# A gated graph network on one core: the late block sums of the matrix as single passes between the first step's gate operations, and waits per bank at the head of step 0

## The chip, the cores and the metric

The kernel runs on 1 core of one Trainium2 chip. The metric is the device time of one execution in microseconds (us). A core has a matrix engine (PE, with weight loads listed apart as PEld), a vector engine (DVE), a scalar engine (ACT), a general engine (POOL) and a queue engine that starts transfers (SP). Each works through its own instructions in order and meets the others only at semaphores.

## The reference

```python
Af, AfT = A.astype(float32), A.astype(float32).T          # 2048 x 2048, zeros and ones
for _ in range(5):
    s_in, s_out = state @ in_W.T + in_b, state @ out_W.T + out_b      # state: 2048 x 256
    a_in, a_out = Af @ s_in, AfT @ s_out
    a = concatenate([a_in, a_out, state], axis=-1)
    r = sigmoid(a @ r_W.T + r_b)
    z = sigmoid(a @ z_W.T + z_b)
    h_hat = tanh(concatenate([a_in, a_out, r * state], axis=-1) @ h_W.T + h_b)
    state = (1.0 - z) * state + z * h_hat
out = tanh(state @ o1_W.T + o1_b) @ o2_W.T + o2_b
x = layernorm(x + out)
```

## The kernel before

The input weights are folded into the gate weights at the start, so a step needs only the products of A and of its transpose with the state, and the bias part of them is the row and column sums of A ("degrees") times a vector. All operands of PE are a high and a low f16 part, made by a `..._hi` operation on ACT and a `..._lo` operation on DVE.

**Streaming, step 0's products.** SP loads 32 row blocks of 1 MB, 16 of A and 16 of its transpose, into a ring of three stages (`load_rows`, k = 0 to 31). ACT casts each to fp8 into `areg` (`cast_rows`), which also gives the degrees. PE multiplies each block with the state into all eight banks. The blocks 14 and 15 of a matrix are kept for last and done bank by bank. For the transpose, column slice c and feature half f have the bank `p0_bank(c, f)`: banks 4, 5, 6, 7, 0, 1, 2, 3 in order. Each is emptied by `p0_hi` (before: the loop at L397 to L399) and `p0_lo` (L659). Between them PE spreads the degrees (`spread_degrees`, L1058) as one row each over banks 4 to 7, d = 0 for A and d = 1 for the transpose. `deg_out` (L719) copies them to `deg`.

**Gates.** A step has four column slices c of 512 nodes; n = 4 t + c counts them over steps. A slice has six gate tiles gi: two of r, two of z, two of h, each 18 matmuls of 128x512 on the banks 4, 5, 6 in turn (`gate_bank`). A bank is seeded with its degree parts first, one by ACT (`seed`, L451) and one by DVE (`degree_part`, L755, which releases the tile through `s_c1`). `gate_act` (L437) applies the sigmoid or tanh; `reset_part`, `reset_lo`, `keep_part` and `update` (L778, L781) are DVE's. `split_hi` (L408) and `split_lo` (L730) make the state operand of a slice, which its first tile needs. In step 0 PE turns finished slices around between tiles (`transposes`, L1176), and ACT and DVE make row operands of them (`rows_hi`, `row_sums`, `rows_lo` L737).

**Steps 1 to 4** multiply in blocks with seven products instead of eight, in four `group`s a step (L1075, 112 matmuls each). For these the matrix blocks' sums and differences are needed. `matrix_sums(i)` makes them on DVE, four passes (L651, L652, L654, L656) for each of 16 jobs; POOL stores them to `kept`. Eleven jobs stand in the streaming stage, the last five (`GATE_JOBS`) in step 0: one before the first `update` of each slice, the fifth after slice 3. SP loads a group's operands from `kept` into `areg` by `load_group`. The load for group 1 of step 1 waits until all sixteen jobs are stored.

The matmuls of groups 0 and 1, then the gates of slices 0 and 1, then groups 2 and 3 and slices 2 and 3 follow in each step. Behind the last slice stand its output head (`last_split_hi` L487, `last_split_lo` L845, `head_hidden` L1188, `head_out` L1207) and the layer norm.

## Time and profile before

| | |
|---|---|
| runs of the kernel before | 1072.14, 1072.59, 1076.05 us (median 1072.59) |
| profiled execution | 1071.97 us, its span 1070.0 us |
| PE busy | 1026.6 us, 96% |
| DVE, ACT busy | 594.9 us (56%), 414.5 us (39%) |
| POOL busy | 37.3 us (3%) |
| transfers | 119.63 MB |

The busy time says how long an engine had an instruction in work, not that it was needed then. The span runs from the first to the last instruction of the profile; 1.97 us of the profiled execution lie around it. Idle time of PE stands in brackets at the row that ends it, with what released it.

### The profile page before, as it was taken

The page shows a single profiled execution, that of the slowest core. Times are in us where ns is not written, and L with a number is a line of the kernel's source. Part 1 is how long each engine was busy: PE and PEld are TensorE (multiplying, and loading weights), DVE is VectorE, ACT ScalarE, POOL GpSimd, SP SyncE. Part 2 cuts the span into 40 slices and gives each one's busy share as a digit, 9 for nine tenths or more (in the row PEclk, how much of TensorE's full clock was granted, in tenths as well). Part 3 has the DMA queues.
Part 4 walks back from the last instruction along what each step waited for, and adds up shares of the span by engine and source line. Part 5 has one row for each costly group of instructions (what it writes and reads, how often), then busy time and mean ns, then how long its engine had stood idle before and what let it go on. Part 6 is the DMA issues. An engine that isn't in the chain of part 4 may idle for free.

```text
span 1070.0 us, 11716 instructions
## 1 busy us (share of the span) xinstructions
PE 1026.6 (96%) x4776; PEld 474.3 (44%) x4776; DVE 594.9 (56%) x924; ACT 414.5 (39%) x551; POOL 37.3 (3%) x44
## 2 busy tenths in 40 slices
PE   7999979998799999999999999999999999999994
PEld 3444434444344444444444444444444444444442
DVE  5999857777335336643543474344337544446755
ACT  3665545543124215521421462244126413322442
POOL 0311000000000000000000000000000001101100
PEclk9999989999899999999999999999999999999997
DMA  9999960000730033004103300330240035001101
GB/s 337 394 384 385 386 244 20 20 20 21 294 138 1 1 138 138 1 17 177 83 1 138 138 1 1 138 138 1 100 176 1 1 138 182 1 1 40 40 1 40
DMA packets 28869, 119.63 MB, mean 112 GB/s; under 512 B 2064, under 2 KB 17040, under 8 KB 20624
## 3 DMA queue, kind: packets, MB, share of 16 engines
q1 hardware_dynamic: 25968, 109.98, 26.8%
q0 software_dynamic: 2304, 8.39, 2.0%
q8 instruction: 37, 0.61, 0.2%
q10 hardware_dynamic: 544, 0.52, 0.1%
q14 instruction: 16, 0.13, 0.0%
HBM read 102.11 MB, written 16.78 MB: 111 GB/s over the span
## 4 chain that ended last, share of the span: by engine, by line
PE 88%; DVE 4%; DMA 2%; ACT 2%; issue 2%; SPq 1%; ACTq 0%; DVEq 0%
PE bank L1163 41%; PE bank L1075 34%; PE bank L1018 10%; PE bank L1176 1%; DMA areg<-kept_operands 1%; DMA tmp<-in_adj 1%; PE bank L1207 1%; PE bank L1188 1%; ACT xop_words L429 0%; DVE deg_words L719 0%; DVE tmp L654 0%; DVE tmp L652 0%; DVE tmp L651 0%; SPq L245 0%; ACT bank L451 0%
## 5 line engine op out<-in xcount | busy, mean ns | idle before, releaser
L1075 PE MATMUL bank<-areg,xop_words 128*128 128x512 fp8e4 x1792 | 392.9, 381 | 6.8 <-DMA areg<-kept_operands 5.4
L1163 PE MATMUL bank<-pq_words,w 128*128 128x512 f16 x1440 | 328.9, 380 | 0.0
L1075 PEld LDWEIGHTS bank<-areg,xop_words 128*128 128x128 f16 x1792 | 175.0, 98 | 219.8 <-DMA areg<-kept_operands 5.9
L1163 PEld LDWEIGHTS bank<-pq_words,w 128*128 128x128 f16 x1440 | 141.3, 98 | 170.0 <-issue 2.5
L437 ACT ACTIVATE tmp<-bank,bias_sb,scal 128x512 f32<-128x512 f32 x120 | 93.3, 777 | 219.7 <-PE bank L1163 211.4
L1163 PE MATMUL bank<-split,w 128*128 128x512 f16 x480 | 119.2, 385 | 11.4 <-DVE split L730 6.8
L755 DVE SCALAR_TENSOR_TENSOR bank<-deg_words,vdeg,bank 128x512 f32<-128x512 f16 x120 | 90.0, 752 | 63.5 <-ACT bank L451 62.3
L517 ACT ACTIVATE pq_words<-pq_words 128x512 f16<-128x512 f32 x48 | 30.2, 630 | 237.1 <-DVE pq_words L925 140.8
L1018 PE MATMUL bank<-areg,xop_words 128*128 128x512 fp8e4 x512 | 113.5, 383 | 2.7 <-ACT areg L377 2.7
L451 ACT ACTIVATE bank<-deg_words,vdeg 128x512 f32<-128x512 f16 x120 | 82.7, 691 | 5.4 <-DVE deg_words L719 1.7
L1018 PEld LDWEIGHTS bank<-areg,xop_words 128*128 128x128 f16 x512 | 50.0, 98 | 65.5 <-issue 7.7
L1163 PEld LDWEIGHTS bank<-split,w 128*128 128x128 f16 x480 | 47.2, 99 | 66.0 <-issue 9.5
L377 ACT ACTIVATE areg<-tmp 128x2048 fp8e4<-128x2048 int32 x32 | 61.1, 1911 | 38.5 <-DMA tmp<-in_adj_t 21.9
L761 DVE TENSOR_TENSOR tmp<-tmp,state_t 128x512 f32<-128x512 f32 x40 | 27.6, 691 | 62.2 <-ACT tmp L437 62.1
L1163 PE MATMUL bank<-tmp,w 128*128 128x512 f16 x240 | 58.3, 379 | 0.0
L939 DVE SCALAR_TENSOR_TENSOR pq_words<-pq_words 128x512 f16<-128x512 f32 x48 | 33.2, 692 | 33.4 <-ACT pq_words L517 33.4
L737 DVE SCALAR_TENSOR_TENSOR xop_words<-pq_words,scal,xop_words 128x512 f16<-128x512 f32 (+1 forms) x32 | 36.8, 1150 | 25.0 <-ACT xop_words L429 25.0
L778 DVE TENSOR_TENSOR tmp<-tmp 128x512 f32<-128x512 f32 x40 | 27.8, 694 | 37.4 <-ACT tmp L437 37.4
L360 POOL TENSOR_TENSOR areg<-areg,diag_words 128x256 f32<-128x256 f32 x16 | 14.2, 918 | 731.3 <-DMA areg<-in_x 731.3
L730 DVE SCALAR_TENSOR_TENSOR split<-state_t,scal,split 128x1024 f16<-128x1024 f32 x23 | 29.5, 1284 | 13.0 <-ACT split L408 12.8
L1163 PEld LDWEIGHTS bank<-tmp,w 128*128 128x128 f16 x240 | 23.5, 98 | 28.3
L429 ACT ACTIVATE xop_words<-pq_words,scal 128x512 f16<-128x512 f32 (+1 forms) x32 | 33.1, 1036 | 7.0 <-DVE pq_words L750 6.5
(118 smaller groups left out, 619.6 us busy)
## 6 DMA issues: line engine op xcount, KB each, us to landing
areg<-kept_operands SPq DMA_DIRECT2D x32, 1792.0 KB, 10.7
tmp<-in_adj SPq DMA_DIRECT2D x16, 1024.0 KB, 6.9
tmp<-in_adj_t SPq DMA_DIRECT2D x16, 1024.0 KB, 8.8
kept_operands<-xop_words POOLq DMA_DIRECT2D x11, 512.0 KB, 8.6
areg<-in_x SPq DMA_DIRECT2D x8, 512.0 KB, 8.0
kept_operands<-areg SPq DMA_DIRECT2D x4, 1024.0 KB, 9.6
kept_operands<-tmp POOLq DMA_DIRECT2D x5, 512.0 KB, 3.1
pq_words<-in_gate_w SPq DMA_DIRECT2D x6, 384.0 KB, 5.8
```

The costliest lines, as they stand in the source:

```text
L377: nc.scalar.activation(raw8[k // JT][:, k % JT, :], stage[:, k % STG, :], ACT.Copy, accum_out=degc[:, k // JT, k % JT:k % JT + 1], saturat ...
L429: nc.scalar.activation(xop[:, xs, 0, 2 * c:2 * c + 2, :], stg[:, bs, :], ACT.Identity, scale=SIGX) \
L437: nc.scalar.activation(dst[:, gi % FT, :], gate_bank[gi % 3][:, :], ACT.Tanh if gi >= 2 * FT else ACT.Sigmoid, bias=bias_sb[:, 4 + gi:5 + ...
L451: nc.scalar.activation(gate_bank[gi % 3][:, :], deg[:, 0, cols(c)], ACT.Identity, scale=vdeg[:, 0, gi:gi + 1]).then_inc(s_c0, 1)
L517: nc.scalar.activation(dst, src, ACT.Copy, scale=PSC / XDOWN).then_inc(s_yh, 1)
L730: nc.vector.scalar_tensor_tensor(split[:, c % 2, 1, :, :], state_t[:, :, cols(c)], SIG, split[:, c % 2, 0, :, :], ALU.mult, ALU.subtract). ...
L737: nc.vector.scalar_tensor_tensor(xop[:, xs, 1, 2 * c:2 * c + 2, :], stg[:, bs, :], SIGX, xop[:, xs, 0, 2 * c:2 * c + 2, :], ALU.mult, ALU. ...
L755: nc.vector.scalar_tensor_tensor(slot, deg[:, 1, cols(c)], vdeg[:, 1, gi:gi + 1], slot, ALU.mult, ALU.add).then_inc(s_c1, 1)
L939: nc.vector.scalar_tensor_tensor(rows[:, 1, :], src, PSC / XDOWN, rows[:, 0, :], ALU.mult, ALU.subtract).then_inc(s_yl, 1)
L1018: return nc.tensor.matmul(dst[:, :], state_n[:, j, part, feat(f)], adj8[:, j, cols(c)], start=j == 0 and part == 0, stop=j == JT - 1 and p ...
L1075: last = nc.tensor.matmul(dst[:, :], xop[:, xo, part, m, :], slot8[g % 2][:, m, mo, :], start=first and m == pairs[0] and part == 0, stop= ...
L1163: last = nc.tensor.matmul(dst[:, :], w16[:, k, wp, feat(gi)], rhs, start=False, stop=i == KT - 1 and (wp, xp) == PASSES[-1], skip_group_ch ...
```

## The change

It has five parts. (1) In `matrix_sum` the four passes of a late job stand apart, and `late_sum` puts them singly at five places of each slice's DVE operations in step 0, 20 passes in 20 places; all five jobs now end inside slice 3. (2) The first `split_hi(0, 0, 0)` stands in ACT's cast stream behind block 26 and its `split_lo` before `make_diag(1)`. (3) The degree rows of A are copied by ACT, those of the transpose by DVE, with a semaphore each (`s_deg_in`, `s_deg_out`), and seeds wait for the copy of their own bank; the banks of slices 2 and 3 are emptied after the seeds. (4) The load of `ow` stands behind block 12 instead of block 17. (5) In the last slice `last_split_hi(0)` stands before the last tile's activation instead of behind it.

```diff
--- before.py
+++ after.py
...
-                if k == JT + 1:
+                if k == JT - 4:
                     sp.dma_start(ow, o_w.rearrange("(k p) m -> p k m", p=P)).then_inc(s_ow, 16)
...
-            for k in range(JT + 1, 2 * JT):
-                cast_rows(k)
-            for c in range(CH):
-                for f in range(FT):
-                    act.wait_ge(s_p0, 2 * c + f + 1)
-                    nc.scalar.activation(pq[:, c, f, 0, :], bank[p0_bank(c, f)][:, :], ACT.Copy, scale=PSC) \
-                        .then_inc(s_p0h, 1)
...
             def split_hi(c, at, new):
+                if at == 0:
+                    for f in range(FT):
+                        act.wait_ge(s_xt[f], 32)
...
-                    if t == LAST and c == CH - 1 and gi == 5:
-                        last_split_hi(0)
-                        last_split_hi(1)
+                    if t == LAST and c == CH - 1 and gi >= 4:
+                        last_split_hi(gi - 4)
...
+            def p0_hi(c, f):
+                act.wait_ge(s_p0, 2 * c + f + 1)
+                nc.scalar.activation(pq[:, c, f, 0, :], bank[p0_bank(c, f)][:, :], ACT.Copy, scale=PSC) \
+                    .then_inc(s_p0h, 1)
+
+            for k in range(JT + 1, 2 * JT):
+                cast_rows(k)
+                if k == JT + 10:
+                    split_hi(0, 0, 0)
             act.wait_ge(s_bias, 16)
-            act.wait_ge(s_deg, 2 * CH)
+            for c in range(CH // 2):
+                for f in range(FT):
+                    p0_hi(c, f)
+            for c in range(CH):
+                act.wait_ge(s_dg, c + 1)
+                nc.scalar.copy(deg[:, 0, cols(c)], bank[4 + c][:, :]).then_inc(s_deg_in, 1)
+            act.wait_ge(s_deg_in, CH)
             for gi in range(3):
+                act.wait_ge(s_deg_out, gi + 1)
                 seed(0, 0, gi)
-            for f in range(FT):
-                act.wait_ge(s_xt[f], 32)
-            split_hi(0, 0, 0)
+            for c in range(CH // 2, CH):
+                for f in range(FT):
+                    p0_hi(c, f)
             for c in range(CH):
                 gates(0, c)
...
-            def matrix_sums(i):
+            def matrix_sum(i, which):
...
-                dve.wait_ge(s_cast, JT * d + 2 * m + 2)
...
-                nc.vector.tensor_tensor(t1, even[:, :, 1, :], even[:, :, 0, :], ALU.subtract, saturate=False).then_inc(s_tc, 1)
-                nc.vector.tensor_tensor(t3, odd[:, :, 1, :], even[:, :, 1, :], ALU.subtract, saturate=False)
-                dve.wait_ge(s_tc, 2 * i + 1)
-                nc.vector.tensor_tensor(t2, odd[:, :, 1, :], t1, ALU.subtract, saturate=False).then_inc(s_tc, 1)
-                dve.wait_ge(s_tc, 2 * i + 2)
-                nc.vector.tensor_tensor(t4, odd[:, :, 0, :], t2, ALU.subtract, saturate=False).then_inc(s_t, 1)
+                if which == 1:
+                    dve.wait_ge(s_cast, JT * d + 2 * m + 2)
+                    if 3 <= i < RING_A:
+                        dve.wait_ge(s_kept_a[i % 3], 16 * (i // 3))
+                    if i >= RING_A + 2:
+                        dve.wait_ge(s_kept_b[(i - RING_A) % 2], 16 * ((i - RING_A) // 2))
+                    nc.vector.tensor_tensor(t1, even[:, :, 1, :], even[:, :, 0, :], ALU.subtract, saturate=False) \
+                        .then_inc(s_tc, 1)
+                if which == 3:
+                    nc.vector.tensor_tensor(t3, odd[:, :, 1, :], even[:, :, 1, :], ALU.subtract, saturate=False)
+                if which == 2:
+                    dve.wait_ge(s_tc, 2 * i + 1)
+                    nc.vector.tensor_tensor(t2, odd[:, :, 1, :], t1, ALU.subtract, saturate=False).then_inc(s_tc, 1)
+                if which == 4:
+                    dve.wait_ge(s_tc, 2 * i + 2)
+                    nc.vector.tensor_tensor(t4, odd[:, :, 0, :], t2, ALU.subtract, saturate=False).then_inc(s_t, 1)
...
+            def late_sum(n, place):
+                k = 5 * n + place
+                if k < 4 * GATE_JOBS:
+                    matrix_sum(RING_A + k // 4, (1, 3, 2, 4)[k % 4])
...
-            for i in range(PAIRS, RING_A):
-                matrix_sums(i)
-            make_diag(1)
-
-            def p0_lo(c, f):
-                dve.wait_ge(s_p0h, 2 * c + f + 1)
-                lo_of_psum(c, f, bank[p0_bank(c, f)], s_p0l)
-
-            def deg_out(d):
-                for c in range(CH):
-                    dve.wait_ge(s_dg, CH * d + c + 1)
-                    nc.vector.tensor_copy(deg[:, d, cols(c)], bank[4 + c][:, :]).then_inc(s_deg, 1)
-
-            for c in range(CH):
-                p0_lo(c, 0)
-                if c >= CH - 2:
-                    deg_out(c - (CH - 2))
-                p0_lo(c, 1)
-            dve.wait_ge(s_deg, 2 * CH)
-
             def split_lo(c, at):
                 dve.wait_ge(s_sph, at + 1)
                 nc.vector.scalar_tensor_tensor(split[:, c % 2, 1, :, :], state_t[:, :, cols(c)], SIG,
                                                split[:, c % 2, 0, :, :], ALU.mult, ALU.subtract).then_inc(s_spl, 1)
...
+            for i in range(PAIRS, RING_A):
+                matrix_sums(i)
+            split_lo(0, 0)
+            make_diag(1)
+
+            def p0_lo(c, f):
+                dve.wait_ge(s_p0h, 2 * c + f + 1)
+                lo_of_psum(c, f, bank[p0_bank(c, f)], s_p0l)
+
+            for c in range(CH // 2):
+                for f in range(FT):
+                    p0_lo(c, f)
+            for c in range(CH):
+                dve.wait_ge(s_dg, CH + c + 1)
+                nc.vector.tensor_copy(deg[:, 1, cols(c)], bank[4 + c][:, :]).then_inc(s_deg_out, 1)
+            dve.wait_ge(s_deg_out, CH)
...
                 reset_lo(n, 0)
                 between(0)
+                if t == 0:
+                    late_sum(n, 0)
...
                 reset_lo(n, 1)
                 between(1)
+                if t == 0:
+                    late_sum(n, 1)
                 degree_part(n, c, 5)
...
                 if t == 0 and c + 1 < CH:
                     split_lo(c + 1, split_at(t, c + 1))
                 between(3)
+                if t == 0:
+                    late_sum(n, 2)
                 keep_part(n, c, 1)
                 if t == 0:
-                    for i in range(RING_A + c, RING_A + c + 1):
-                        matrix_sums(i)
+                    late_sum(n, 3)
                 if t == LAST and c == CH - 1:
                     head_split(2)
                 update(n, c, 0)
                 between(4)
                 if ahead:
                     degree_part(n + 1, (c + 1) % CH, 1)
+                if t == 0:
+                    late_sum(n, 4)
                 if c == CH - 1 and t < LAST:
                     rows_lo(n, 0)
...
             for gi in range(3):
                 degree_part(0, 0, gi)
-            split_lo(0, 0)
+            for c in range(CH // 2, CH):
+                for f in range(FT):
+                    p0_lo(c, f)
             for c in range(CH):
                 gates(0, c)
-                if c == CH - 1:
-                    for i in range(RING_A + CH, len(TJOBS)):
-                        matrix_sums(i)
...
                         pe.wait_ge(s_p0h, c + 1)
                         pe.wait_ge(s_p0l, c + 1)
                     else:
-                        pe.wait_ge(s_deg, c + 1)
+                        pe.wait_ge(s_deg_in, c + 1)
...
                 if n == 0 and f == 0:
-                    pe.wait_ge(s_deg, 2 * CH)
+                    pe.wait_ge(s_deg_out, CH)
...
```

The first place is the head of step 0 on DVE. Before, from `make_diag(1)` (L665) on, DVE has the parts of the products' banks (L659), both sets of degree rows (L719), the three degree parts of the gate banks (L755) and the split (L730) in this order:

```order
L665 TENSOR_SCALAR tmp<-ident,degc 128x128 x16
L659 SCALAR_TENSOR_TENSOR pq_words<-bank,pq_words 128x512 x5
L719 CAST deg_words<-bank 128x512 x4
L659 SCALAR_TENSOR_TENSOR pq_words<-bank,pq_words 128x512 x2
L719 CAST deg_words<-bank 128x512 x4
L659 SCALAR_TENSOR_TENSOR pq_words<-bank,pq_words 128x512
L755 SCALAR_TENSOR_TENSOR bank<-deg_words,vdeg,bank 128x512 x3
L730 SCALAR_TENSOR_TENSOR split<-state_t,scal,split 128x1024
```

In the changed kernel the same place reads:

```order
L735 SCALAR_TENSOR_TENSOR split<-state_t,scal,split 128x1024
L690 TENSOR_SCALAR tmp<-ident,degc 128x128 x16
L684 SCALAR_TENSOR_TENSOR pq_words<-bank,pq_words 128x512 x4
L752 CAST deg_words<-bank 128x512 x4
L777 SCALAR_TENSOR_TENSOR bank<-deg_words,vdeg,bank 128x512 x3
L684 SCALAR_TENSOR_TENSOR pq_words<-bank,pq_words 128x512 x4
```

The split moved ahead of everything, four of the eight degree copies are gone from DVE, and four of the eight bank parts moved behind the three degree parts.

The second place is the same one on ACT. Before:

```order
L377 ACTIVATE areg,degc<-tmp 128x2048 x15
L399 ACTIVATE pq_words<-bank 128x512 x8
L451 ACTIVATE bank<-deg_words,vdeg 128x512 x3
L408 ACTIVATE split<-state_t,scal 128x1024
L437 ACT_TABLE_LOAD
```

And in the changed kernel:

```order
L377 ACTIVATE areg,degc<-tmp 128x2048 x10
L403 ACTIVATE split<-state_t,scal 128x1024
L377 ACTIVATE areg,degc<-tmp 128x2048 x5
L532 ACTIVATE pq_words<-bank 128x512 x4
L545 CAST deg_words<-bank 128x512 x4
L446 ACTIVATE bank<-deg_words,vdeg 128x512 x3
L532 ACTIVATE pq_words<-bank 128x512 x4
L432 ACT_TABLE_LOAD
```

The split stands between the casts, the copies of the first degree rows came over from DVE, and half of the banks are emptied behind the seeds.

The third place is slice 1 of step 0 on DVE, from the split of slice 2 to the degree part (bank 5) that the second gate tile of slice 2 waits for. Before:

```order
L730 SCALAR_TENSOR_TENSOR split<-state_t,scal,split 128x1024
L737 SCALAR_TENSOR_TENSOR xop_words<-pq_words,scal,xop_words 128x5x256
L772 SCALAR_TENSOR_TENSOR tmp<-tmp,state_t 128x512
L651 TENSOR_TENSOR tmp<-areg 128x2x512
L652 TENSOR_TENSOR tmp<-areg 128x2x512
L654 TENSOR_TENSOR tmp<-areg,tmp 128x2x512
L656 TENSOR_TENSOR tmp<-areg,tmp 128x2x512
L778 TENSOR_TENSOR tmp<-tmp 128x512
L781 TENSOR_TENSOR state_t<-tmp 128x512
L755 SCALAR_TENSOR_TENSOR bank5<-deg_words,vdeg,bank5 128x512
```

In the changed kernel:

```order
L735 SCALAR_TENSOR_TENSOR split<-state_t,scal,split 128x1024
L759 SCALAR_TENSOR_TENSOR xop_words<-pq_words,scal,xop_words 128x5x256
L671 TENSOR_TENSOR tmp<-areg,tmp 128x2x512
L794 SCALAR_TENSOR_TENSOR tmp<-tmp,state_t 128x512
L662 TENSOR_TENSOR tmp<-areg 128x2x512
L800 TENSOR_TENSOR tmp<-tmp 128x512
L803 TENSOR_TENSOR state_t<-tmp 128x512
L777 SCALAR_TENSOR_TENSOR bank5<-deg_words,vdeg,bank5 128x512
L665 TENSOR_TENSOR tmp<-areg 128x2x512
```

Two passes instead of four stand ahead of the update; another one stands behind the degree part. Two further ones of the slice stand earlier, at the reset operations.

## Rows read from the trace of the kernel before

**Rows 1.** The page: busy us (share of the span) and instructions of each engine.

```profile
PE 1026.6 (96%) x4776; PEld 474.3 (44%) x4776; DVE 594.9 (56%) x924; ACT 414.5 (39%) x551; POOL 37.3 (3%) x44
```

**Rows 2.** Stretches: us, busy time by engine, PEclk, DMA share, GB/s.

```profile
143.20:147.00 3.80, 3.78 (x9) 1.34 (x10) 0.00 (x0) 0.00 (x0) 0.00 (x0) 0.50 0.94 368
...
309.00:1045.00 736.00, 735.15 (x3475) 341.02 (x3474) 358.80 (x551) 264.13 (x363) 14.21 (x16) 1.00 0.18 70
```

**Rows 3.** PE in order of time: start, us, what, in brackets idle before.

```profile
133.93 1.01 PE L1058 MATMUL bank<-tmp,ones 128*128 128x512 f16 x3
...
143.22 2.72 PE L1163 MATMUL bank<-split,w 128*128 128x512 f16 x6 [6.82 <-DVE split L730]
...
149.03 1.46 PE L1163 MATMUL bank<-split,w 128*128 128x512 f16 x6
...
198.99 1.47 PE L1163 MATMUL bank<-split,w 128*128 128x512 f16 x6 [2.30 <-DVE bank L755]
...
225.65 2.74 PE L1163 MATMUL bank<-split,w 128*128 128x512 f16 x6 [2.31 <-DVE bank L755]
...
231.21 0.60 PE L1176 MATMUL bank<-ident,state_t 128*128 128x128 f32 x4
...
251.08 0.66 PE L1176 MATMUL bank<-ident,state_t 128*128 128x128 f32 x4 [3.29 <-DVE state_t L781]
...
269.11 8.04 PE L1075 MATMUL bank<-areg,xop_words 128*128 128x512 fp8e4 x36 [0.54 <-DVE pq_words L913]
282.54 26.58 PE L1075 MATMUL bank<-areg,xop_words 128*128 128x512 fp8e4 x112 [5.39 <-DMA areg<-kept_operands]
```

**Rows 4.** The chain of work, in order of time: start, us, what.

```profile
268.16 3.15 DMA kept_operands<-tmp
...
271.82 10.68 DMA areg<-kept_operands
...
309.12 46.62 PE bank L1163 x216
```

**Rows 5.** ACT in order of time, from the last cast to the split.

```profile
124.02 1.91 ACT L377 ACTIVATE areg<-tmp 128x2048 fp8e4<-128x2048 int32 x1 [2.56 <-DMA tmp<-in_adj_t]
...
127.93 0.60 ACT L399 ACTIVATE pq_words<-bank 128x512 f16<-128x512 f32 x1 [1.91 <-PE bank L1018]
...
138.77 1.91 ACT L451 ACTIVATE bank<-deg_words,vdeg 128x512 f32<-128x512 f16 x3 [1.73 <-DVE deg_words L719]
140.62 1.13 ACT L408 ACTIVATE split<-state_t,scal 128x1024 f16<-128x1024 f32 x1
```

**Rows 6.** DVE in order of time, at the head of step 0 and in slice 1.

```profile
132.62 2.47 DVE L719 CAST deg_words<-bank 128x512 f16<-128x512 f32 x4
...
139.57 2.07 DVE L755 SCALAR_TENSOR_TENSOR bank<-deg_words,vdeg,bank 128x512 f32<-128x512 f16 x3 [0.30 <-ACT bank L451]
141.79 1.28 DVE L730 SCALAR_TENSOR_TENSOR split<-state_t,scal,split 128x1024 f16<-128x1024 f32 x1
...
190.12 1.55 DVE L737 SCALAR_TENSOR_TENSOR xop_words<-pq_words,scal,xop_words 128x1280 f16<-128x1280 f32 x1
...
192.19 1.22 DVE L651 TENSOR_TENSOR tmp<-areg 128x1024 fp8e4<-128x1024 fp8e4 x1
...
195.71 1.22 DVE L656 TENSOR_TENSOR tmp<-areg,tmp 128x1024 fp8e4<-128x1024 fp8e4 x1
196.85 0.68 DVE L778 TENSOR_TENSOR tmp<-tmp 128x512 f32<-128x512 f32 x1
```

**Rows 7.** DVE in order of time, the last slice's first update and split.

```profile
1043.35 0.69 DVE L781 TENSOR_TENSOR state_t<-tmp 128x512 f32<-128x512 f32 x1
1047.12 0.75 DVE L845 SCALAR_TENSOR_TENSOR split<-state_t,scal,split 128x512 f16<-128x512 f32 x1 [3.08 <-ACT split L487]
```

**Rows 8.** ACT's and PE's part in the same place, each in order of time.

```profile
1046.38 0.71 ACT L487 ACTIVATE split<-state_t,scal 128x512 f16<-128x512 f32 x1
...
1050.79 1.47 PE L1188 MATMUL bank<-split,o 128*128 128x512 f16 x6 [1.22 <-DVE split L845]
```

17 lines of the change are left out of this document (8 added, 9 removed).

## Prediction

> **What bounds the kernel now.** I read the page first: PE is busy for 96% of the span, so time can only come from what PE waits for or runs slowly [rows 1]. Then the stretches. From 309 to 1045 us PE is busy 735.15 of 736 us at the full granted clock (2.4 GHz); nothing is to be had there, and whatever PE gains before 309 us moves all of it forward [rows 2]. Then PE in order of time, for its gaps. Between the end of streaming and group 1 of step 1 there are six: 6.82, 2.30, 2.31, 3.29, 0.54 and 5.39 us [rows 3], and one of 1.22 us in the tail [rows 8]. A bracket understates the loss a little: six matmuls take 1.46 us as a row but follow each other every 0.216 us (46.62 us for 216 in the chain), so the last one's end lies 0.16 us behind the time at which the next could have started [rows 3, 4]. I add 0.16 us to each gap.
>
> Some gaps have a second price, the clock. After the gap of 6.82 us PE ran at 0.50 of full speed, which is the 1.2 GHz level, for 3.8 us [rows 2]; the 18 matmuls of that tile took 5.81 us instead of 3.89. After the second 2.31 us gap a tile took 5.56 us (lost: 1.67), and the 112 matmuls after the 5.39 us gap took 26.42 instead of 24.17 (lost: 2.25). After the gaps of 2.30, 3.29 and 0.54 us nothing was lost [rows 3].
>
> **The change, part by part.**
>
> Head of step 0. Before, PE waits for a serial chain: four degree copies on DVE, the seeds on ACT, the split on ACT at 140.62, the split on DVE at 141.79 [rows 5, 6]. In the changed kernel both halves of the split are long done. What is left: PE starts the transpose's degree matmuls at 133.93, one every 0.216 us [rows 3]. The first is done at 134.31 and the fourth, without the wait for DVE's copies of A's degrees that it had, at 134.96. DVE, free by then, copies four in 2.47 us, 134.33 to 136.80, and waits for all of them. ACT's seeds need only their own bank's copy and A's degrees; three take 1.91 us from 135.0 on, and the first is there in time. The first degree part takes 0.75 us (three took 2.07) [rows 6], to 137.6, and releases PE. That is 143.22 - 137.6 = **5.6 us** earlier. PE's last product matmuls end at about 135.8, so a gap of 1.7 us is left. It is shorter than all gaps that cost clock, so I count the **1.9 us** too. A's degree copies on ACT have no row; the nearest is ACT's emptying of a bank, 0.60 us, beside 0.62 us for DVE's copy. Started at once they are done before PE asks; started as late as DVE started them (132.62) they end at 135.1 and PE loses 0.5 us. I take 0, since ACT has nothing else then. The four bank parts behind the seeds (4 x 0.60 on ACT, 4 x 0.6 on DVE) lie under the first tile's 3.89 us; nobody needs them before slice 2. Were they not covered, they would cost 2.4 us once.
>
> The split inside the cast stream (1.13 us, behind block 26) delays the next cast. ACT sat idle for 2.56 us before block 31's cast, waiting for its transfer [rows 5], so the stream follows the transfers and ACT has room. Block 31 is cast at 126.0 and PE's first use of it starts about 1.0 us before the 127.93 at which the first bank is emptied, at 126.9: a slack of 0.9 us. Cost 0, at worst 0.3. The load of `ow` (0.5 MB) only changes places with other loads, and the casts there run ahead of PE: 0. The DVE split falls into the idle time before `make_diag(1)`, which waits for that last cast: 0.
>
> Late sums. In slice 1 DVE spends 192.19 to 196.85 on four passes, 1.17 us each, before it can do the update whose degree part releases PE at 198.99 [rows 3, 6]. The changed order has two passes there (one before and one after `keep_part`). The update then starts at 196.85 - 2.33 = 194.52 and PE is released at 196.66, against 196.53 at which it is free. Of 2.46 us, 0.13 stay: **2.3 us**. Slice 2 repeats this: **2.3 us**, and with a gap of 0.1 us no slow tile, **1.7 us**. The fifth pass stands behind that degree part; the next degree part has a whole tile (3.89 us) of room. The passes at the reset operations are followed by operands that the h tiles need four tiles later. In slice 3 the turn of the new state waits for the same update: 3.45 us become 1.1, **2.3 us**. Its other half is covered by 24 matmuls.
>
> The last job. Before, it stands behind slice 3; its store starts at 268.16, takes 3.15 us, and the load for group 1 takes 10.68, so PE gets it at 282.54 [rows 3, 4]. Now its last pass ends inside slice 3, just behind the degree part that follows the update. In the old times of slice 3 that update ends at 251.08 - 2.3 = 248.8; with a degree part (0.75) and the pass (1.17) it is 250.7. From the old store to PE's start are 14.4 us, so the load has landed by about 265.4. Group 0 ended at 269.11 + 36 x 0.216 = 276.9 and now ends 2.3 us earlier on that scale, at 274.6. So the load has 9 us of room, and the gap of 5.55 us goes: **5.6 us**, and the slow stretch behind it, **2.2 us**. DVE no longer has four passes in front of group 0's sums; of that gap of 0.70 us I take **0.4 us** (0 to 0.7).
>
> The tail. The split of the last slice's first half waited for ACT until 1047.12 although its state was ready at 1044.04, because ACT did it behind the last tile's activation [rows 7, 8]. Done at 1044.1 it takes 0.71 us on ACT and 0.75 on DVE, both over by 1045.5, before the last tile's activation can start. The second update then starts 0.64 + 0.67 us earlier, and PE waited 1.22 + 0.16 us for its split: **1.3 us**.
>
> **Sum.** 5.6 + 1.9 + 2.3 + 2.3 + 1.7 + 2.3 + 5.6 + 2.2 + 0.4 + 1.3 = 25.6 us. The profiled execution took 1071.97 us, so 1046.4 us. The median of the runs lies 0.6 us above the profiled execution, so I predict 1047.0 us for the runs.
>
> Is the clock term safe? The Trainium skill ("TensorE: Matmul & The Clock Gate", section "What's actually happening") says that the low clock is the default which activity lifts, and that where the slow matmuls fall varies from run to run. The trace agrees that equal gaps are paid unequally (2.30 us: nothing, 2.31 us: 1.67 us). [...]
>
> **The rivals.**
>
> (a) The head gap or slice 3's gap keeps its slow clock: 1.9 us less, 1048.9. For it: two gaps of almost one length were paid differently. Against: none below 2.31 us was paid. The mechanism is an activity-dependent clock that any gap may trip.
>
> (b) DVE stays the bound in step 0. Its chain from the next slice's split to the update depends on ACT's split, and I find 0.1 us of room. If one more pass of 1.17 us falls in front of the update or the degree part in each of three slices, 3.5 us are lost and slice 2's slow tile may stay: 25.6 - 3.5 - 1.7 = 20.4, so 1052.2.
>
> (c) The split and reordering at the head do not help, since PE finds another wait there (ACT's copies late, or casts held up): the 7.5 us of the head stay, 1054.5. Against it is that each step of that chain has its row.
>
> (d) The load for group 1 is still late, because another store or the queue holds it. Then 5.6 + 2.2 us stay, 1054.8. Against it are 9 us of room.
>
> (e) Slower. The first split waits in ACT's stream for the state's own transfer, and behind it stand five casts; with a ring of three stages SP's loads stop too. Each us beyond the 0.9 us of slack is a us of PE. It would have to come 32 us late to outweigh 25.6 us and 5.4 more, so after block 31 has been cast; then 1078. That transfer is issued before the loads of the blocks 24 to 26, which the casts wait for anyway, so it is most unlikely. Short of that, it eats part of the gain: case (c).
>
> (f) No change to be measured: the waits only move to other places of PE's path. For this all 20 passes would have to stand in PE's way: 23.4 us, against 8.4 that the passes of slices 1 to 3 cost before, so 15.0 us more. The terms of the head (7.5), the last job (7.8), group 0's sums (0.4) and the tail (1.3) are 17.0, which leaves 2.0 us of gain, 1070.6. But four passes at one place cost PE only 2.46 us of their 4.66 before, and a slice has 6 x 3.89 = 23.3 us of tiles for its 5.9 us of passes, so I give it little.
>
> **How the numbers follow.** The forecast with all terms, 0.62; (a) 0.14; (b) 0.12; (c) and (d) together 0.08; (f) 0.03; (e) 0.01. The range reaches up to (b): high end 1052.0. Low end: the other 0.3 us at group 0's sums, slice 3's further 1.1 and the small 0.13s are 1.6 us, so 1045.0. A measurement of this kernel can tell about 0.5% (5.4 us) from no change. Faster by more than that: all of the forecast and (a) to (d), 0.96; within it 0.03; slower 0.01.
>
> **What would show it.** In the changed trace PE's first gate tile starts near 137.6, with an idle time of about 1.5 us before it ended by a degree part and not by a split. The first row of a slice's second tile carries no bracket above 0.3 us in slices 2 and 3. The turn before step 1 waits about 1 us. The last store of the sums is issued before PE starts group 0, and group 1 has no wait for a transfer. PE's whole clock rises. In the tail PE goes from the first half of the hidden product to the second with no wait. I am wrong if the gaps of DVE's making come back with a degree part as their releaser, or if a tile before 300 us runs at 1.2 GHz after a gap below 2 us.

## The result, and the profile after

| | median us | runs | ratio to before, 95% interval |
|---|---|---|---|
| before, on the same chip | 1073.72 | 4 (1072.14 to 1076.05) | |
| changed | 1046.72 | 4 (1046.11 to 1046.90) | 0.9746 [0.9725, 0.9767] |
| changed, once more beside later experiments | 1045.58 | 4 (1044.01 to 1047.40) | 0.9728 [0.9705, 0.9751] |

The kernel is 2.5% faster. The forecast was 1047.0 us, in a range of 1045.0 to 1052.0. The profiled execution took 1046.88 us and its span 1044.9, so the span is 25.1 us shorter than before; the sum of the terms was 25.6.

The page of the changed kernel: busy time of each engine, the granted clock of PE in the 40 slices of the span (tenths), and the chain's shares. They answer to [rows 1].

```profile
PE 1019.8 (98%) x4776; PEld 473.5 (45%) x4776; DVE 592.2 (57%) x920; ACT 415.6 (40%) x555; POOL 37.7 (4%) x44
...
PEclk8999999999999999999999999999999999999997
...
PE 94%; DVE 2%; ACT 1%; DMA 1%; issue 1%; SPq 1%; ACTq 0%; DVEq 0%
```

PE has the same 4776 matmuls and is busy 6.8 us less for them, 5.8 of it because three stretches ran at the high clock where they had run at the low one (1.93 + 1.66 + 2.25), the rest from the 0.16 us that a row's end adds before each gap. The rest of the 25.1 us is idle time. PE in order of time, from the head of step 0 to the turn, then group 0 and the load behind it, then the tail:

```profile
134.95 1.03 PE L1046 MATMUL bank<-areg,xop_words 128*128 128x512 fp8e4 x4
137.89 1.46 PE L1191 MATMUL bank<-split,w 128*128 128x512 f16 x6 [1.91 <-issue]
139.18 2.75 PE L1191 MATMUL bank<-pq_words,w 128*128 128x512 f16 x12
141.77 1.46 PE L1191 MATMUL bank<-split,w 128*128 128x512 f16 x6
...
185.38 1.46 PE L1191 MATMUL bank<-split,w 128*128 128x512 f16 x6
...
189.34 1.47 PE L1191 MATMUL bank<-split,w 128*128 128x512 f16 x6
...
213.72 1.47 PE L1191 MATMUL bank<-split,w 128*128 128x512 f16 x6
...
217.62 0.60 PE L1204 MATMUL bank<-ident,state_t 128*128 128x128 f32 x4
...
235.21 0.66 PE L1204 MATMUL bank<-ident,state_t 128*128 128x128 f32 x4 [0.90 <-DVE state_t L803]
...
252.99 32.22 PE L1103 MATMUL bank<-areg,xop_words 128*128 128x512 fp8e4 x148 [0.29 <-DVE pq_words L942]
285.05 1.46 PE L1191 MATMUL bank<-split,w 128*128 128x512 f16 x6
...
1024.21 2.88 PE L1216 MATMUL bank<-split,o 128*128 128x512 f16 x12
1029.78 4.42 PE L1235 MATMUL bank<-o,pq_words 128*128 128x256 f16 x24 [2.69 <-DVE pq_words L883]
```

Beside [rows 3] and [rows 8]: the six gaps between streaming and group 1 have become three, of 1.91, 0.90 and 0.29 us. The second tiles of slices 2 and 3 (189.34 and 213.72) carry no bracket. Groups 0 and 1 stand in one row of 148 matmuls, since nothing came between them. In the tail the twelve matmuls of the hidden product have become one row. Cut at the same instructions in both traces, the span divides so (the last matmul of a row counts 0.216 us, as in the prediction, so groups 0 and 1 end at 282.54 + 26.58 - 0.16 = 308.96 in the trace of before, where PE's next row starts):

| stretch, between starts of PE's rows | before | after | saved | term in the sum |
|---|---|---|---|---|
| start to the first gate tile | 143.22 | 137.89 | 5.33 | 5.6 |
| that tile | 5.81 | 3.88 | 1.93 | 1.9 |
| to slice 2's second tile | 49.96 | 47.57 | 2.39 | 2.3 |
| to slice 3's second tile | 26.66 | 24.38 | 2.28 | 2.3 |
| that tile, to the transposes | 5.56 | 3.90 | 1.66 | 1.7 |
| to the turn of the new state | 19.87 | 17.59 | 2.28 | 2.3 |
| to group 0 | 18.03 | 17.78 | 0.25 | 0.4 |
| groups 0 and 1 | 39.85 | 32.06 | 7.79 | 5.6 + 2.2 |
| to the second half of the last hidden product | 741.83 | 740.46 | 1.37 | 1.3 |
| to the end | 19.21 | 19.39 | -0.18 | 0 |
| sum | | | 25.10 | 25.6 |

DVE at the head of step 0 and in slice 1, in order of time, answers to [rows 6]:

```profile
134.51 2.48 DVE L752 CAST deg_words<-bank 128x512 f16<-128x512 f32 x4 [2.50 <-PE bank L1086]
137.03 2.07 DVE L777 SCALAR_TENSOR_TENSOR bank<-deg_words,vdeg,bank 128x512 f32<-128x512 f16 x3
...
181.66 1.28 DVE L735 SCALAR_TENSOR_TENSOR split<-state_t,scal,split 128x1024 f16<-128x1024 f32 x1 [1.57 <-ACT split L403]
182.87 1.55 DVE L759 SCALAR_TENSOR_TENSOR xop_words<-pq_words,scal,xop_words 128x1280 f16<-128x1280 f32 x1
184.33 1.22 DVE L671 TENSOR_TENSOR tmp<-areg,tmp 128x1024 fp8e4<-128x1024 fp8e4 x1
185.46 0.69 DVE L794 SCALAR_TENSOR_TENSOR tmp<-tmp,state_t 128x512 f32<-128x512 f32 x1
186.07 1.22 DVE L662 TENSOR_TENSOR tmp<-areg 128x1024 fp8e4<-128x1024 fp8e4 x1
187.20 0.69 DVE L800 TENSOR_TENSOR tmp<-tmp 128x512 f32<-128x512 f32 x1
187.92 0.69 DVE L803 TENSOR_TENSOR state_t<-tmp 128x512 f32<-128x512 f32 x1
188.53 0.75 DVE L777 SCALAR_TENSOR_TENSOR bank<-deg_words,vdeg,bank 128x512 f32<-128x512 f16 x1
```

Of the 5.33 us at the first gate tile, streaming took 0.16 back: the transpose's degree matmuls began at 134.09 here and at 133.93 before. The copies of the transpose's degrees start at 134.51 and the first degree part is done at 137.03 + 0.75 = 137.78, 0.11 us before PE starts its tile. In slice 1 two passes (L671 and L662) stand ahead of the update, and the degree part ends at 189.28. PE's first tile of slice 2 started at 185.38 and takes 18 x 0.216 = 3.89 us, so PE was free at 189.27. From its last wait (for ACT's split, until 181.66) to the end of the degree part DVE has 7.62 us of work, and PE was free 7.61 us after that wait: DVE has no room here. PE starts 0.07 us late.

ACT at the head, in order of time, answers to [rows 5], and POOL's last store to [rows 4]:

```profile
124.10 1.91 ACT L377 ACTIVATE areg<-tmp 128x2048 fp8e4<-128x2048 int32 x1 [1.32 <-DMA tmp<-in_adj_t]
...
131.76 2.05 ACT L545 CAST deg_words<-bank 128x512 f16<-128x512 f32 x4 [0.48 <-PE bank L1086]
135.29 1.91 ACT L446 ACTIVATE bank<-deg_words,vdeg 128x512 f32<-128x512 f16 x3 [1.48 <-DVE deg_words L752]
...
237.25 0.72 POOL L347 DMA_DIRECT2D kept_operands<-tmp  x1 [16.16 <-DVE tmp L671]
```

The last store of the sums leaves at 237.25, where it had started at 268.16. SP issues the load for group 1 at 240.54; the DMA engines' busy share is 0.77 from 250 to 251 us and 0.00 from 251 to 256, so it had landed by 251. Group 0 ends at about 252.99 + 36 x 0.216 = 260.8, which leaves over 9 us of room, as forecast.

### The profile page after: what moved, and what is told of

The parts are those of the page before. It is cut to its first block, busy times and chain, and to the rows that moved or that the text cites. A ratio compares the mean times of both kernels' runs of the same rounds, so it can differ in the third digit from the quotient of the medians.

```text
span 1044.9 us, 11717 instructions
## 1 busy us (share of the span) xinstructions
PE 1019.8 (98%) x4776; PEld 473.5 (45%) x4776; DVE 592.2 (57%) x920; ACT 415.6 (40%) x555; POOL 37.7 (4%) x44
## 4 chain that ended last, share of the span: by engine, by line
PE 94%; DVE 2%; ACT 1%; DMA 1%; issue 1%; SPq 1%; ACTq 0%; DVEq 0%
PE bank L1191 44%; PE bank L1103 36%; PE bank L1046 11%; PE bank L1204 1%; DMA tmp<-in_adj 1%; PE bank L1235 1%; PE bank L1216 1%; SPq L245 0%; DVE areg L903 0%; DVE pq_words L942 0%; DVE ln_st L895 0%; ACT pq_words L511 0%; ACT areg L579 0%; ACT areg L377 0%; PE bank L1086 0%
## 5 line engine op out<-in xcount | busy, mean ns | idle before, releaser
L1191 PE MATMUL bank<-split,w 128*128 128x512 f16 x480 | 116.7, 379 | 1.9 <-issue 1.9
```

The costliest lines, as they stand in the source:

```text
L1191: last = nc.tensor.matmul(dst[:, :], w16[:, k, wp, feat(gi)], rhs, start=False, stop=i == KT - 1 and (wp, xp) == PASSES[-1], skip_group_ch ...
```

## The experiments

The first five change the kernel before, the next five the changed kernel. Each has its own interval against the kernel before.

**The single passes alone** (part 1).

```diff
                 between(0)
+                if t == 0:
+                    late_sum(n, 0)
...
                 keep_part(n, c, 1)
                 if t == 0:
-                    for i in range(RING_A + c, RING_A + c + 1):
-                        matrix_sums(i)
+                    late_sum(n, 3)
...
                 for c in range(CH):
                     gates(0, c)
-                    if c == CH - 1:
-                        for i in range(RING_A + CH, len(TJOBS)):
-                            matrix_sums(i)
```

> The kernel before with part 1 alone (single passes). Theory (gains add, each read from its gap): slices 2 and 3 start their second tile 2.4 us earlier each, the slow tile behind the second gap goes (1.7), slice 3's turn comes 2.4 us earlier, group 0's sums 0.4, the transfer wait before group 1 goes with its slow stretch (5.6 + 2.2): 16.7 us faster than the kernel before. Rival (the clock's losses hang on the moment, not on the gaps): one or both slow stretches stay, 12.8 to 15 us. Rival (head and passes depend on each other, DVE has room only after the shorter head): under 10 us.

Measured: 1055.37 us (4 runs, 1054.70 to 1058.28), beside a median of 1073.67 for before (14 runs), ratio 0.9839 [0.9808, 0.9870]. The profiled span is 1052.7 us, 17.3 less than before's, of which 0.9 are from a streaming stage that ended earlier. All of PE's gaps from the gate stage to group 1, in order of time:

```profile
142.33 2.72 PE L1182 MATMUL bank<-split,w 128*128 128x512 f16 x6 [6.82 <-DVE split L745]
241.77 0.66 PE L1195 MATMUL bank<-ident,state_t 128*128 128x128 f32 x4 [0.90 <-DVE state_t L796]
259.55 32.21 PE L1094 MATMUL bank<-areg,xop_words 128*128 128x512 fp8e4 x148 [0.28 <-DVE pq_words L935]
```

The head's gap is as before, at the low clock. The five others are those of the changed kernel: 0.90, 0.28, and three that are gone. Part 1 gives two thirds of the whole (18.3 of 27.0 us by the medians). The expected 16.7 us lie inside the interval.

**The head alone** (parts 2, 3 and 4).

```diff
+                if k == JT + 10:
+                    split_hi(0, 0, 0)
...
+            for c in range(CH):
+                act.wait_ge(s_dg, c + 1)
+                nc.scalar.copy(deg[:, 0, cols(c)], bank[4 + c][:, :]).then_inc(s_deg_in, 1)
...
+            split_lo(0, 0)
             make_diag(1)
```

> The kernel before with the parts at the head and in the stream (2, 3, 4) alone. Theory: PE's first gate tile starts 5.3 us earlier and is not slow (1.9): 7.2 us faster, and the four later gaps of 2.3, 2.3, 3.3 and 5.4 us stay as they are. Rival (the gain at the head is given back at the load for group 1 or at DVE): 0 to 3 us. Rival (the first tile is slow all the same or another one gets slow): 5.3 us or less.

Measured: 1067.54 us (5 runs, 1065.97 to 1068.26), ratio 0.9938 [0.9918, 0.9959]; profiled span 1065.7, 4.3 less than before's. PE's gaps:

```profile
137.39 1.45 PE L1173 MATMUL bank<-split,w 128*128 128x512 f16 x6 [1.91 <-issue]
191.23 2.60 PE L1173 MATMUL bank<-split,w 128*128 128x512 f16 x6 [2.31 <-DVE bank L763]
219.58 1.47 PE L1173 MATMUL bank<-split,w 128*128 128x512 f16 x6 [2.31 <-DVE bank L763]
243.34 1.11 PE L1186 MATMUL bank<-ident,state_t 128*128 128x128 f32 x4 [3.29 <-DVE state_t L789]
244.25 7.92 PE L1085 MATMUL bank<-areg,xop_words 128*128 128x512 fp8e4 x24
```

The head behaves as in the changed kernel: a gap of 1.91 us and a fast first tile. Yet the other gaps were paid differently than before. In slice 2 the tile after 2.31 us now ran slow, in slice 3 the same gap cost nothing, and behind the 3.29 us gap, which had been free, the transposes took 1.11 instead of 0.66 us and the 24 matmuls after them 7.92 instead of 5.34. Cut like the table above, the head gives 5.83 + 1.93 us, slice 2 takes 1.69 back, slice 3 returns 1.66, the stretch behind the 3.29 us gap takes 3.01 and groups 0 and 1 take 0.75 (the wait for the load is 5.70 us and its slow stretch a little longer). So the span gained less than the head's own 7 us: what it lacks lies at gaps that this kernel keeps. The second half of the third rival, another tile gets slow, is what this execution shows.

**The tail alone** (part 5).

```diff
-                    if t == LAST and c == CH - 1 and gi == 5:
-                        last_split_hi(0)
-                        last_split_hi(1)
+                    if t == LAST and c == CH - 1 and gi >= 4:
+                        last_split_hi(gi - 4)
```

> The kernel before with part 5 alone (the last slice's first split ahead of the last activation). Theory: PE's gap of 1.2 us before the second half of the hidden product goes, 1.3 us faster. Rival (DVE's residual rows are in the way anyway): 0.

Measured: 1072.56 us (10 runs, 1069.21 to 1074.89), ratio 0.9985 [0.9966, 1.0005]. The runs alone don't show it. The trace shows the edit's mechanism (span 1067.2):

```profile
1048.12 2.88 PE L1187 MATMUL bank<-split,o 128*128 128x512 f16 x12
1053.68 2.78 PE L1206 MATMUL bank<-o,pq_words 128*128 128x256 f16 x24 [2.69 <-DVE pq_words L853]
```

The two halves are one row, so the gap of 1.22 us is gone [rows 8]. The last 24 matmuls took 2.78 us here; in the kernel before they took 4.45 and in the changed one 4.42, behind the same gap of 2.69 us. So about 1.4 us of the span's 2.8 are the edit's.

**The last jobs earlier, in whole.** Is it the single passes or only their earlier place that frees the load? Here the four passes stay together, but each job stands one place earlier, the first in DVE's idle time at the head.

```diff
-                    for i in range(RING_A + c, RING_A + c + 1):
-                        matrix_sums(i)
+                    matrix_sums(RING_A + c + 1)
...
             split_lo(0, 0)
+            matrix_sums(RING_A)
             for c in range(CH):
                 gates(0, c)
-                if c == CH - 1:
-                    for i in range(RING_A + CH, len(TJOBS)):
-                        matrix_sums(i)
```

> The kernel before with its four-pass jobs left whole, but each one place earlier: the first stands on DVE ahead of slice 0's gate operations (where DVE is idle for 7 us), the others before the first update of slices 0 to 3, none behind slice 3. Theory: the gaps of slices 1 to 3 stay (2.3, 2.3, 3.3), the wait for the load of group 1 goes with its slow stretch (5.6 + 2.2) and 0.4 us at group 0's sums: 8.2 us faster. Rival (it takes single passes): under 1 us. If the slow stretch stays, 6.0 us.

Measured: 1064.31 us (4 runs, 1062.83 to 1066.42), ratio 0.9915 [0.9886, 0.9943]; profiled span 1063.0.

```profile
198.80 2.74 PE L1160 MATMUL bank<-split,w 128*128 128x512 f16 x6 [2.31 <-DVE bank L755]
227.04 1.47 PE L1160 MATMUL bank<-split,w 128*128 128x512 f16 x6 [2.31 <-DVE bank L755]
250.80 1.11 PE L1173 MATMUL bank<-ident,state_t 128*128 128x128 f32 x4 [3.29 <-DVE state_t L781]
```

The gaps of 2.31, 2.31 and 3.29 us are those of before within 0.01 us, and group 1 waits for no transfer: PE does groups 0 and 1 in one row again. By the medians the gain is 9.4 us where 8.2 were expected, inside the interval. So part 1 has two mechanisms. That the last job ends earlier takes the load off the path, whatever the passes look like. That no more than two passes stand ahead of an update takes off the three gaps.

**The first split alone** (part 2).

```diff
+            for k in range(JT + 1, 2 * JT):
+                cast_rows(k)
+                if k == JT + 10:
+                    split_hi(0, 0, 0)
...
+            split_lo(0, 0)
             make_diag(1)
```

> The kernel before with part 2 alone: the first split stands in the cast stream, the degree copies and bank parts stay as they were. Theory (the head is a serial chain of which the split is the last 2.8 us): PE's first gate tile is released by the first degree part at 140.4 us instead of by the split at 143.2, so 2.8 us faster, and the gap falls from 6.8 to 4.0 us; its first tile may still be slow (then no more is gained) or not (1.9 more). Rival (the split in the stream holds the casts up by its 1.1 us): 1.7 us or less, and the last cast ends later than before. Rival (the degree copies' order does it all): 0.

Measured: 1070.77 us (10 runs, 1068.19 to 1074.16) beside 1073.84, ratio 0.9974 [0.9956, 0.9992]; profiled span 1065.9.

```profile
140.00 2.72 PE L1165 MATMUL bank<-split,w 128*128 128x512 f16 x6 [4.03 <-issue]
195.19 1.47 PE L1165 MATMUL bank<-split,w 128*128 128x512 f16 x6 [2.30 <-DVE bank L758]
221.85 1.47 PE L1165 MATMUL bank<-split,w 128*128 128x512 f16 x6 [2.31 <-DVE bank L758]
```

The head's gap shrinks by 2.79 us, from 6.82 to 4.03, and is still paid at the low clock (2.72 for six matmuls). The split is 2.8 of the head's 7.3 us. The rest is left for the copies' new engines and order (part 3) and the earlier load of `ow` (part 4); no run has either of them by itself. Behind the split ACT sat idle for 2.22 us before the last cast, so the cast stream was not held up.

**One pass more ahead of the update** (in the changed kernel). If DVE has no more room than 0.1 us, a third pass there is paid in full, three times.

```diff
                 if t == 0:
                     late_sum(n, 3)
+                    late_sum(n, 4)
...
                     degree_part(n + 1, (c + 1) % CH, 1)
-                if t == 0:
-                    late_sum(n, 4)
```

> The changed kernel with the fifth pass of each slice of step 0 moved from behind the degree part to ahead of the update, so that three passes stand there instead of two. Theory (DVE has 0.1 us of room at slices 2 and 3 and none at the turn): the second tiles of slices 2 and 3 wait 1.2 us each and the turn 2.1 us instead of 0.9, together 3.4 us slower than the changed kernel; a gap may also cost slow matmuls, up to 1.9 us each. Rival (DVE has room of a pass): 0.

Measured: 1049.90 us (4 runs, 1049.29 to 1051.83) beside 1075.14, ratio 0.9777 [0.9752, 0.9802]; profiled span 1047.3.

```profile
189.67 1.47 PE L1190 MATMUL bank<-split,w 128*128 128x512 f16 x6 [1.05 <-DVE bank L777]
215.08 1.47 PE L1190 MATMUL bank<-split,w 128*128 128x512 f16 x6 [1.05 <-DVE bank L777]
237.70 0.66 PE L1203 MATMUL bank<-ident,state_t 128*128 128x128 f32 x4 [2.15 <-DVE state_t L803]
```

Gaps of 1.05, 1.05 and, at the turn, 2.15 instead of 0.90 us. From the first gate tile to the end the trace is 3.2 us longer than the changed kernel's (910.2 and 907.0 us), where 3.4 were expected. Rival (b)'s price per slice was right; what the changed order avoids is exactly this third pass. The tiles behind these gaps kept the high clock.

**A degree part behind its own bank's copy.** In the changed kernel DVE copies four banks before the first degree part. Here each degree part stands behind the next bank's copy.

```diff
                 nc.vector.tensor_copy(deg[:, 1, cols(c)], bank[4 + c][:, :]).then_inc(s_deg_out, 1)
+                if c > 0:
+                    dve.wait_ge(s_deg_out, c)
+                    first_degree_part(c - 1)
```

> The changed kernel with the three degree parts of slice 0 each behind the copy of its own bank instead of behind all four copies. Theory: the first degree part starts behind the first seed, at about 136.0 instead of 137.0 us, so PE's first gate tile starts 1.1 us earlier and the gap falls from 1.9 to 0.8 us: 1.1 us faster than the changed kernel. Rival (PE waits for something else at its head, its own queue or the banks): 0.

Measured: 1045.18 us (4 runs, 1045.08 to 1046.37), ratio 0.9730 [0.9710, 0.9750]. The gap at the head is 0.94 us shorter, where 1.1 was expected:

```profile
137.60 1.46 PE L1199 MATMUL bank<-split,w 128*128 128x512 f16 x6 [0.97 <-issue]
...
136.74 0.75 DVE L754 SCALAR_TENSOR_TENSOR bank<-deg_words,vdeg,bank 128x512 f32<-128x512 f16 x1 [0.30 <-ACT bank L446]
```

The first degree part now waits for ACT's seed and ends at 137.49, again 0.11 us before PE starts. So it is this degree part that PE waits for at its head, though the bracket names no releaser (`issue`). The medians alone don't separate this kernel from the changed one.

**No pass between `keep_part` and the update.** The passes are spread 8, 4, 4 and 4 over the slices. Slices 1 to 3 have two at the reset operations, one behind the first `keep_part` and one behind the degree part that follows the update.

```diff
+            LATE = ((1, 1, 2, 1, 1, 2), (1, 1, 1, 0, 0, 1), (1, 1, 1, 0, 0, 1), (1, 1, 1, 0, 0, 1))
+            late_done = [0]
...
             def late_sum(n, place):
-                k = 5 * n + place
-                if k < 4 * GATE_JOBS:
+                for _ in range(LATE[n][place]):
+                    k = late_done[0]
                     matrix_sum(RING_A + k // 4, (1, 3, 2, 4)[k % 4])
+                    late_done[0] += 1
```

> The changed kernel with the same 20 passes in other places: eight in slice 0, and four in each later slice (two at the reset operations, one behind the first keep_part, one behind the degree part), none ahead of the update. Theory: the 0.9 us gap at the turn and the four small ones (0.1 us each) go: 1.4 us faster than the changed kernel. Rival (the new place behind keep_part delays the next degree part or the split and makes gaps of its own): 0 or slower.

Measured: 1044.67 us (4 runs, 1043.31 to 1046.11), ratio 0.9723 [0.9701, 0.9744]; profiled span 1041.9. After the head's 1.90 us PE has one bracket left up to 300 us; the 0.90 us at the turn is gone:

```profile
250.03 32.21 PE L1109 MATMUL bank<-areg,xop_words 128*128 128x512 fp8e4 x148 [0.29 <-DVE pq_words L948]
```

From the first gate tile to the end it is 905.5 us, beside 907.0 in both traces of the changed kernel, so 1.5 us shorter, where 1.4 were expected. The medians alone don't show it.

**The last head rows from other banks.** Half of the residual of slice 2 stood on DVE between PE and its last 24 matmuls. Here it stands behind `head_split`, and the last rows use the banks 6 and 7 for two of their four.

```diff
-                return bank[j][:, 0:D]
+                return bank[(0, 1, 6, 7)[j]][:, 0:D]
...
-            residual(2)
+            residual(2, (0, 1))
             head_split(CH - 1)
+            residual(2, (2, 3))
...
             def head_out(c):
-                if 0 < c:
+                if 0 < c < CH - 1:
                     pe.wait_ge(s_y, JC * c)
```

> The changed kernel with the last head's rows of blocks 2 and 3 in banks 6 and 7, so that PE need not wait for slice 2's residual rows, and half of these rows moved behind head_split(3) on DVE. Theory: the gap of 2.7 us before the last head product falls to 1.4 us: 1.3 us faster than the changed kernel. Rival (the residual rows then stand in the way of the last ones): 0 to 0.5 us.

Measured: 1046.58 us (5 runs, 1043.96 to 1050.47), ratio 0.9740 [0.9716, 0.9765]; profiled span 1047.8. In this execution PE waited in streaming for a late transfer's cast:

```profile
129.81 6.18 PE L1048 MATMUL bank<-areg,xop_words 128*128 128x512 fp8e4 x20 [2.04 <-ACT areg L377]
...
1032.98 2.79 PE L1237 MATMUL bank<-o,pq_words 128*128 128x256 f16 x24 [1.41 <-DVE pq_words L883]
```

The gap fell as expected, to 1.41 instead of 2.69 us, and the 24 matmuls took 2.79 us instead of 4.42. The times alone don't separate this kernel from the changed one. What the gap's 1.28 us are worth depends on the clock behind it. From the start of the last hidden product to the end this trace takes 19.1 us, against 20.7 in both traces of the changed kernel, whose 24 matmuls were slow; but the kernel with the tail alone, which kept the 2.69 us gap and had fast matmuls behind it, took 19.1 as well. Against such an execution the edit gains nothing, and there the rival was right.

**All three** (the last three together) and the changed kernel once more, beside each other.

> The changed kernel with the three further edits together (degree parts per bank at the head, passes moved away from the updates, last head in free banks). Theory (the gaps are in series, so the gains add): 0.9 + 1.4 + 1.3 = 3.6 us faster than the changed kernel, about 1043 us, with one gap of about 1.0 us at the head, 0.3 us in each step's group 0, and 1.4 us in the tail. Rival (later passes or the clock take some of it back): under 2.5 us.

> The changed kernel once more, beside the three edits. Both theories: 1046.7 us, within 1 us.

Measured: 1043.20 us (4 runs, 1042.20 to 1044.04), ratio 0.9705 [0.9684, 0.9725], and 1045.58 us (1044.01 to 1047.40) for the changed kernel, ratio 0.9728 [0.9705, 0.9751]. The profiled spans are 1039.8 and 1043.3. All gaps of the first from 126 to 300 us and its last in the tail:

```profile
135.98 1.46 PE L1207 MATMUL bank<-split,w 128*128 128x512 f16 x6 [0.97 <-issue]
249.56 32.21 PE L1119 MATMUL bank<-areg,xop_words 128*128 128x512 fp8e4 x148 [0.28 <-DVE pq_words L959]
...
1025.07 2.79 PE L1251 MATMUL bank<-o,pq_words 128*128 128x256 f16 x24 [1.41 <-DVE pq_words L899]
```

The changed kernel came 1.1 us below the 1046.7 expected, just outside the 1 us given. The kernel with all three is the fastest of all here by its median, 2.4 us below the changed one run beside it; the intervals of the two ratios overlap, so the size is not sure, and the expected 3.6 us are not told apart from the rival's "under 2.5". The two spans differ by 3.5 us. Cut at the same rows, that is 0.33 us up to the first gate tile (0.94 of it from the gap, less 0.6 because streaming ended later here), 1.52 up to groups 0 and 1, 1.27 at the gap in the tail, and only 0.38 behind it, although the last 24 matmuls took 1.63 us less. Why the fast matmuls gave so little is to be seen on DVE, where the last residual starts. In the changed kernel (second trace) it waits for PE:

```profile
1031.69 0.88 DVE L903 SCALAR_TENSOR_TENSOR areg<-bank,scal,areg 128x256 f32<-128x256 f32 x2 [2.30 <-PE bank L1235]
```

and with all three it waits for nobody:

```profile
1027.88 0.38 DVE L928 BATCH_NORM_AGGREGATE ln_mv<-ln_st 128x2 f32<-128x6 f32 x4
1028.29 0.87 DVE L919 SCALAR_TENSOR_TENSOR areg<-bank,scal,areg 128x256 f32<-128x256 f32 x2
```

The residual rows that moved behind `head_split` now lie between it and the last residual, and DVE became the bound of the tail: the last residual starts 3.22 us after PE's last 24 matmuls do, beside 3.50 in the changed kernel.

## Why the prediction was right

**What bounds the kernel.** Right. Every us that PE gained before 309 us came out at the end, and the stretch behind it kept its length: 741.83 and 740.46 us, and the 1.37 between them are the tail's own edit.

**The head, 5.6 + 1.9.** Measured 5.33 + 1.93. The chain was the forecast one: DVE's four copies, one degree part, PE; the kernel with a degree part behind its own bank's copy confirms the releaser. The tile started at 137.89 instead of 137.6. DVE's copies began at 134.51 and not 134.33, nearly all of it because streaming ended 0.16 us later, and PE needed 0.11 us from the degree part's end to its tile. ACT's copies of A's degrees, which had no row, took 2.05 us for four from 131.76 on and were over at 133.81, before the transpose's degree matmuls at 134.09: cost 0, as taken. The trace with part 2 alone shows why the two edits belong together: the split alone leaves a gap of 4.03 us with its slow tile.

**The late sums, 2.3 + 2.3 + 1.7 + 2.3.** Measured 2.39, 2.28, 1.66 and 2.28. The forecast had 0.13 us left in each slice; 0.07 are left (189.34 against 189.27). The kernel with a third pass shows that this was no luck of rounding: one pass more is paid with 1.05 + 0.16 - 0.07 = 1.14 us in each slice.

**The last job, 5.6 + 2.2.** Measured 7.79 together. The store was issued at 237.25, and the load had landed over 9 us before PE asked for it. (The prediction's 265.4 should be 250.7 + 14.4 = 265.1, which changes nothing.) The kernel with whole jobs one place earlier has this gain without the other one.

**Group 0's sums and the tail, 0.4 + 1.3.** Measured 0.25 and 1.37. The bottom of the range, 1045.0, is a little below what its own terms give: 1047.0 - 1.6 = 1045.4.

**The parts add up.** By their medians, against 1073.67, the parts give 18.3 (passes), 6.1 (head) and 1.1 us (tail), together 25.5, and the changed kernel 27.0 against its own 1073.72. What the sum did not have is how differently the same gap can be paid in the kernel before. Its runs scatter from 1071.43 to 1077.65; the changed kernel's eight from 1044.01 to 1047.40, probably because fewer gaps are left that can be slow or not. The profiled execution of before was one of its cheaper ones (a span of 1070.0 us, where the median over 36 others is 1071.7): it lost nothing behind the gap of 3.29 us, where other kernels lost 1.4 to 3.0 us in three traces of five. By that share (an estimate: 7.3 us lost in five traces) the change is worth about 1.5 us more than the sum says. That the forecast hit the median within 0.3 us is therefore partly luck: the changed kernel's profiled execution took 1046.88 us where the sum gave 1046.4, and its median lies 0.2 us below that execution where 0.6 above was assumed.

**The signs.** All came but for two details: the idle time before the first gate tile is 1.91 us and not about 1.5, and its bracket says `issue` instead of a degree part. None of the signs of being wrong came.

**The rivals.** (a) The head's gap of 1.91 us, or the rests in slices 2 and 3, kept no slow clock in any of the kernels that had them. (b) was the nearest: it asks for one more pass ahead of the update or its degree part, and the changed order has none to spare. The kernel with that pass took 1049.90 and not 1052.2, mostly since its tiles stayed fast. (c), (d), (e) and (f) did not come: the head's chain was as forecast, the load was early, and ACT waited for its transfers (1.32 us before the last cast, 2.22 in the kernel with part 2 alone), not the other way round.

**The clock terms.** They came out, but the ground on which I took them, that the same gap is paid the same way in other executions, does not hold. Gaps of one length and what followed them, in the 13 traces of this case, one of each kernel and two of the changed one:

| idle time of PE | followed by the 1.2 GHz level |
|---|---|
| 0.89 to 2.15 us, behind streaming | 0 of 23 |
| 0.42 and 0.83 us, in streaming | 0 of 2 |
| 2.04 us, in streaming (last head rows from other banks) | 1 of 1 |
| 2.47 to 4.85 us, where streaming begins (at 20 to 22 us) | 12 of 13 |
| 2.30 and 2.31 us | 4 of 10 |
| 2.69 us, in the tail | 9 of 11 |
| 3.29 us | 3 of 5 |
| 4.03 to 6.82 us | 9 of 9 |

The kernel before paid at the second of its 2.3 us gaps; the kernels with the head's edit or with earlier jobs paid at the first, the one with part 2 alone at neither. So each such gap was worth about 0.4 x 1.7 = 0.7 us on average (an estimate from ten gaps), and a single trace shows it as 0 or as 1.7. The total over slices 2 and 3 came out right because the change took away both gaps, and the profiled execution had paid at one of them. Had the change taken away only one, the forecast could have been off by 1.7 us, according to the execution profiled. Nor is the price fixed where it is always paid: the first gate tile lost 1.4 to 2.4 us behind the gaps of 4.03 and 6.82 us. That this is the execution and not only the kernel is to be seen in the runs of the kernel before: over 36 of them the granted clock is 0.979 to 0.987 on average and the span 1069.4 to 1075.4 us, in the main longer where the clock is lower. The Trainium skill ("TensorE: Matmul & The Clock Gate", section "What's actually happening") says that the number of slow matmuls at a kernel's start differs from run to run of one kernel. The table shows the same for gaps far behind the start.

## What to carry to other kernels

Where a vector engine has work that nobody waits for soon, cut it to single instructions and place them behind the operation that releases the bound engine, not ahead of it; then count what stands on that engine from the last thing it waits for to that release, against the time until the bound engine has nothing left to do. Here that was 7.62 against 7.61 us; two passes cost PE 0.07 us per slice and a third 1.14 us more. When a gap closes, ask for its second price too: a slow clock behind a gap of 2.3 to 3.3 us is a chance and not a fixed cost, so take a gap's slow stretch at its share over several traces, also where the one trace you have shows none, and the gap itself in full.

## What the runs showed of the hardware

- Gaps of one length are followed by the low clock in some executions and not in others (table above). In the tail PE did 24 matmuls of 128x256 and 12 of 128x512 before a gap of 2.69 us, and the 24 matmuls after it took 2.78 us in two kernels and 4.38 to 4.45 in nine traces. The twelve came with a gap of 1.22 us in their middle in five traces (one fast, four slow) and without it in six (one fast, five slow). Short gaps were not safe everywhere: the 2.04 us gap in streaming was followed by 20 matmuls in 6.18 us, where 4.48 are usual at the high clock (20 of group 0 in the changed kernel). From 129.8 to 136.0 us the granted clock was 0.72 there on average, after 1.00 up to the gap's end.
- The price of a slow stretch varies too: behind the gap of 3.29 us, from the transposes' start to the next transposes, 8.66, 8.53 and 7.11 us in the three traces that paid, and 5.67 in the two that did not.
- ACT copies a PSUM bank of 128x512 f32 to f16 in less time than DVE: 2.05 us for four, beside 2.48.
- The end of streaming moves from execution to execution without any edit: the first degree matmuls began at 131.35 us in one trace of the changed kernel and at 129.77 in the other. In the kernel with the late transfer they began at 135.82. One or two us between two kernels can only be read from their gaps, or from many runs.
